# Self-attention: output products in the turned probabilities' banks, values of the last tile one head later, next keys odd first, finer waits at scores and output

## What is computed

```python
def _attn(x, ctx, Wq, Wk, Wv, Wo, bo):       # 16 heads of 64, ctx is the normed x itself
    q = (x @ Wq).reshape(b, n, HEADS, DHEAD)
    k = (ctx @ Wk).reshape(b, m, HEADS, DHEAD)
    v = (ctx @ Wv).reshape(b, m, HEADS, DHEAD)
    scale = DHEAD ** (-0.5)
    sim = jnp.einsum('bihd,bjhd->bhij', q, k) * scale
    attn = jax.nn.softmax(sim, axis=-1)
    out = jnp.einsum('bhij,bjhd->bihd', attn, v).reshape(b, n, INNER)
    return out @ Wo + bo
h = _ln(x, g1, be1)
x = _attn(h, h, Wq1, Wk1, Wv1, Wo1, bo1) + x
```

## Time and profile before

| | us |
|---|---|
| median of three executions | 6849.94 (6849.8 to 6850.25) |
| the profiled execution's own time | 6856.39 |
| its span, first to last instruction | 6854.6 |
| PE busy | 6140.2 (90%) |
| POOL busy | 4645.0 (68%) |
| DVE busy | 5100.9 (74%) |
| ACT busy | 3774.8 (55%) |
| self-attention, first scores of batch 0 to the last addition | about 50 to 1283 |
| mean granted clock of PE | 0.947 of full speed |

### The profile page before, as it was taken

The page is one execution under the profiler, slowest core; times in us unless marked ns, Lnnn a source line. Parts: engine busy times, 40 slices in busy tenths (PEclk is TensorE's granted clock), DMA queues, the critical chain, the costliest instruction groups (busy, mean ns, idle before and its releaser), DMA issues. The chain is left out here.

```text
span 6854.6 us, 73694 instructions
## 1 busy us (share of the span) xinstructions
PE 6140.2 (90%) x20586; PEld 2577.3 (38%) x20586; DVE 5100.9 (74%) x5938; ACT 3774.8 (55%) x6915; POOL 4645.0 (68%) x2164
## 2 busy tenths in 40 slices
PE   9999999999998888888888888888888888888898
PEld 4555555544443332323332323333323333323444
DVE  4444444543218999999999999999999999995623
ACT  4444444432226666666666666666666666664532
POOL 3333334223008999999999999999999999993300
PEclk9999999999999999999999999999999999999998
DMA  2000000213003232333232333232333232332000
GB/s 78 0 0 0 0 0 0 83 25 118 0 0 90 63 87 63 87 79 90 63 87 63 87 79 91 63 87 63 87 79 89 63 87 63 86 79 56 5 0 25
DMA packets 228700, 387.51 MB, mean 57 GB/s; under 512 B 46304, under 2 KB 64416, under 8 KB 225936
## 3 DMA queue, kind: packets, MB, share of 16 engines
q1 hardware_dynamic: 228368, 383.75, 23.0%
HBM read 207.14 MB, written 23.40 MB: 34 GB/s over the span
## 5 line engine op out<-in xcount | busy, mean ns | idle before, releaser
L2580 POOL TENSOR_TENSOR work<-work,weights 128x1024 f32<-128x1024 f32 x1152 | 2693.3, 2366 | 14.0 <-PE banks L2444 7.4
L2444 PE MATMUL banks<-work 128*64 128x512 f32 x4608 | 1359.2, 671 | 554.0 <-POOL work L2585 553.7
L2500 DVE TENSOR_TENSOR_SCAN banks<-banks,work 128x512 f32<-128x512 f32 x1368 | 1710.0, 1271 | 41.6 <-ACT banks L2548 41.3
L2548 ACT ACTIVATE banks<-work 128x512 f32<-128x512 f32 x2304 | 1501.1, 680 | 68.6 <-DVE work L2292 43.1
L2500 DVE TENSOR_TENSOR_SCAN work<-banks,work 128x512 f32<-128x512 f32 x936 | 1173.7, 1270 | 98.3 <-ACT banks L2548 70.9
L2585 POOL TENSOR_TENSOR work<-work,weights 128x1024 f32<-128x1024 f32 x468 | 1104.8, 2361 | 160.4 <-ACT work L2167 160.4
L2005 PE MATMUL banks<-work,weights 128*128 128x512 f32 (+31 forms) x3796 | 1147.3, 453 | 3.6 <-DVE work L2265 3.0
L606 POOL TENSOR_TENSOR work<-work 128x1024 f32<-128x1024 f32 x256 | 480.0, 1895 | 778.8 <-DVE work L472 778.4
L2298 DVE TENSOR_TENSOR work<-banks,weights 128x512 f32<-128x512 f32 x1368 | 902.4, 670 | 0.0
L2005 PEld LDWEIGHTS banks<-work,weights 128*128 128x128 f32 x3796 | 636.5, 190 | 605.1 <-issue 526.5
L2444 PEld LDWEIGHTS banks<-work 128*64 128x64 f32 x4608 | 269.1, 144 | 1414.7 <-POOL work L2585 853.8
(11 more groups left out here) (320 smaller groups left out, 7300.2 us busy)
## 6 DMA issues: line engine op xcount, KB each, us to landing
weights<-mamba_bc SPq DMA_DIRECT2D x592, 256.0 KB, 5.0
work<-work SPq DMA_DIRECT2D x1160, 128.0 KB, 2.3
weights<-mamba_taps SPq DMA_DIRECT2D x5, 2048.0 KB, 7.4
weights<-cross_vo SPq DMA_DIRECT2D x16, 512.0 KB, 6.9
mamba_taps<-work SPq DMA_DIRECT2D x4, 2048.0 KB, 6.8
cross_vo<-weights SPq DMA_DIRECT2D x6, 1024.0 KB, 8.9
work<-in_conv_rows SPq DMA_DIRECT2D x16, 256.0 KB, 5.8
out_T<-X SPq DMA_DIRECT2D x8, 512.0 KB, 3.3
```

What stands on the lines that cost most here:

```text
L2444: mm = e.matmul(ybank[k % 2][64 * h:64 * h + 64, :], fold, ring_pair(n, j)[:, h, :], start=False, stop=(a == SP_ - 1))
L2500: e.tensor_tensor_scan(ub if by_pool(j) else da, da, ub, state[:, i:i + 1], ALU.mult, ALU.add).then_inc(scanned, 1)
L2548: e.activation(banks[:, slot_of(i), :], dt_rep[:, k % 2, h, :], ACT.Exp, scale=decay[:, f:f + 1]).then_inc(da_full, 1)
L2580: e.tensor_tensor(ring_pair(n, j), u_rep[:, k % 2], bc[:, a, 0, :].unsqueeze(1).to_broadcast([P, 2, TC]), ALU.mult) \
```

## The change

Five things, all in `self_attention`:

- The output products' tiles go to banks 4 and 5 and have their own semaphore `out_full`; the additions raise `added` instead of `v_free`, and the first `turn` of the next batch waits for it. `V_SHARE` counts two uses of lane V fewer.
- Ahead of the scores PE waits for `V(-1)` and `S(-1)`, all but the last use of each lane; the wait for all of them stands in the first `mix`.
- `VALUES_AT` is a table from beat to token tiles: tiles 0 and 1 in beat 0, tile 2 in beat 1, tile 3 in beat 2 (behind that beat's second turn). DVE and ACT follow the same table.
- The next batch's first four key tiles are made in the order 1, 0, 3, 2.
- Ahead of the output products PE waits for all but the last use of lane S; the product with k = 7 of the first tile waits for the last.

```diff
@@ -284,17 +284,18 @@
     p_ready = core.sem("self_probs")
     t_full = core.sem("self_t_full")
     tv_free, ts_free = core.sem("self_tv_free"), core.sem("self_ts_free")
+    out_full, added = core.sem("self_out"), core.sem("self_added")
     x_in = lambda b: [(P, core.X[:, k, b, PRE:S1]) for k in range(KD)]
     rows = [P] * KD
 
 
     MEAN_HEAD, VARIANCE_HEAD, BIAS_HEADS = 3, 9, (11, 13)
-    KEYS_AHEAD, KEYS_HEAD, VALUES_AT, V_TAKES = 4, H0 - 2, (0, 1), {3: 0, 7: 2, 11: 4, 14: 6}
+    KEYS_AHEAD, KEYS_HEAD, VALUES_AT, V_TAKES = 4, H0 - 2, {0: (0, 1), 1: (2,), 2: (3,)}, {3: 0, 7: 2, 11: 4, 14: 6}
     V_BEGIN, S_BEGIN = 1 + KEYS_AHEAD // 2, 1 + KEYS_AHEAD // 2
-    V_SHARE, S_SHARE = 12 + PAIRS // 2 + 1 + 2, 12 + PAIRS // 2 + 1
+    V_SHARE, S_SHARE = 12 + PAIRS // 2 + 1, 12 + PAIRS // 2 + 1
     v_done = lambda b: b * V_SHARE + (V_BEGIN + 12 - KEYS_AHEAD // 2 + (MEAN_HEAD + 1) // 4 + 1)
     s_done = lambda b: b * S_SHARE + (S_BEGIN + 12 - KEYS_AHEAD // 2 + VARIANCE_HEAD // 4 + 1)
-    out_bank = lambda m: (core.lane_v, core.banks[:, 4, :])[m]
+    out_bank = lambda m: core.banks[:, 4 + m, :]
 
     with core.nc.Block() as block:
         @block.sync
@@ -355,10 +356,13 @@
                     project(wq, m)
                 for m in range(KEYS_AHEAD, 8):
                     project(wk, m)
-                e.wait_ge(ln.v_free, V())
-                e.wait_ge(ln.s_free, S())
+                e.wait_ge(ln.v_free, V(-1))
+                e.wait_ge(ln.s_free, S(-1))
 
                 def mix(g):
+                    if g == 0:
+                        e.wait_ge(ln.v_free, V())
+                        e.wait_ge(ln.s_free, S())
                     e.wait_ge(tv_free, b * (2 * H0) + 2 * (g + 1))
                     e.wait_ge(ts_free, b * (2 * H0) + 2 * (g + 1))
                     lane, free, full, c = lanes[g // 2 % 2]
@@ -376,6 +380,8 @@
 
                 def turn(g, u):
                     e.wait_ge(p_ready, b * (H0 * UNITS) + (g * UNITS + u + 1))
+                    if g == 0 and u == 0:
+                        e.wait_ge(added, b * KD)
                     for j in range(2):
                         e.wait_ge((tv_free, ts_free)[j], b * (2 * H0) + (2 * g + u))
                         for kt in range(4):
@@ -405,8 +411,8 @@
                     if g >= 1:
                         mix(g - 1)
                     if h in VALUES_AT:
-                        for t in range(2):
-                            project_values(2 * VALUES_AT.index(h) + t)
+                        for t in VALUES_AT[h]:
+                            project_values(t)
                     if g < 0:
                         continue
                     if more and g == MEAN_HEAD:
@@ -415,16 +421,17 @@
                         norm_variance_pe(e, core, nm, ln, S, b + 1, x_in(b + 1), core.mean_d, squared, T)
                     if more and g == KEYS_HEAD:
                         e.wait_ge(nm.ready, b + 2)
-                        for m in range(KEYS_AHEAD):
+                        for m in (1, 0, 3, 2):
                             project(wk, m)
                 mix(H0 - 1)
                 e.wait_ge(ln.v_free, V())
-                e.wait_ge(ln.s_free, S())
+                e.wait_ge(ln.s_free, S(-1))
                 for m in range(KD):
                     for k in range(8):
+                        if m == 0 and k == 7:
+                            e.wait_ge(ln.s_free, S())
                         mm = e.matmul(out_bank(m), wo[:, k, m * P:(m + 1) * P], q[:, k, :], start=(k == 0), stop=(k == 7))
-                    mm.then_inc(ln.v_full, 1)
-                    V.add()
+                    mm.then_inc(out_full, 1)
 
             batches(e, body)
 
@@ -488,7 +495,7 @@
                     if h < H0:
                         reciprocal(h, 0)
                     if h in VALUES_AT:
-                        for t in range(2 * VALUES_AT.index(h), 2 * VALUES_AT.index(h) + 2):
+                        for t in VALUES_AT[h]:
                             e.wait_ge(ln.v_full, V(1))
                             e.tensor_copy(v_[:, t, 0:512], core.lane_v).then_inc(ln.v_free, 1)
                             V.add()
@@ -506,11 +513,10 @@
                                                           in1=core.lane_s, op0=ALU.mult, op1=ALU.mult)
                         last.then_inc(ln.s_free, 1)
                 for m in range(KD):
-                    e.wait_ge(ln.v_full, V(1))
+                    e.wait_ge(out_full, b * KD + m + 1)
                     x = core.X[:, m, b, PRE:S1]
                     e.scalar_tensor_tensor(out=x, in0=out_bank(m), scalar=core.v("bo1", m), in1=x,
-                                           op0=ALU.add, op1=ALU.add).then_inc(ln.v_free, 1)
-                    V.add()
+                                           op0=ALU.add, op1=ALU.add).then_inc(added, 1)
 
             batches(e, body)
 
```

## The result

| | us |
|---|---|
| before, median of 4 executions | 6850.09 (6849.8 to 6860.37) |
| changed, median of 4 executions | 6814.43 (6810.55 to 6822.56) |
| ratio changed to before | 0.9943, 95% interval 0.9931 to 0.9956 |
| changed, the profiled execution | 6822.56, span 6820.7 |

What follows compares the result with a forecast made beforehand. PE was taken to bound the self-attention, so only its gaps could shrink. The sum 7 x 1.23 + 8 x 0.76 + 8 x 1.52 + 7 x 0.61 + 8 x 0.77 = 37.4 us took 6849.94 to 6812.5; range 6805 to 6823.

Steps and rivals of the forecast that it cites:

- (a): Output products in banks 4 and 5: next batch's queries no longer wait for DVE's additions; 1.23 us, seven times.
- (c): Values of tile 3 moved to head 2, between two turns, so the second no longer waits for DVE; 1.52 us, eight times.
- slow restart: At a turn that follows a wait: 0.03 us extra, counted within the gain of (c).
- rival 1: Only part comes: the second turn at (c) still waits, leaving 25.2 us gained, 6824.7 us; chance 0.06.
- (b): Scores wait only for the last key but one, not ACT's copy of key tile 7; 0.76 us, eight times.
- (e): Output products start before ACT has taken the last pair; 0.77 us, eight times.
- (d): Next batch's keys in the order 1, 0, 3, 2: gain 0.86, net 0.61 us after DVE's delay, seven times.
- DVE's delay at head 15: DVE copies the last key before its turned copy, so PE's turn waits 0.25 us longer; taken off (d).
- the idle column: Pricing waits by PE's recorded idle time alone: 34.2 us, 32.4 after DVE's delay, the lower bound; time 6817.5.
- Rival 3: The waits only move: PE arrives earlier at the probabilities and waits for POOL; 6837.5 us if two thirds eaten; chance 0.04.
- Rival 4: Gaps at (a) and (e) are the queue's own and stay: 22.6 us gained, 6827.3 us; chance 0.03.
- the sign of being wrong on the whole: Behind the self-attention's barrier: a stage changing by more than 4 us would show the whole forecast wrong.

Runs made afterwards that it cites:

- both waits covered: The mix of head 13 put between head 14's turns, keys 3 and 2 between head 15's, against the changed kernel; median 6806.24 us.

## Why the prediction was right

The bound, the five places and their prices held. Per batch the forecast was 4.89 us and the trace shows 4.97. That the median came within 2 us of 6812.5 is in part luck: the four executions of the changed kernel spread over 12.0 us, two profiles of it differ by 0.4 us in the self-attention and by 5.1 behind it, and a longer wait for the loads in batch 0 (1.4 us) was not in the sum. The length of a batch is what bears the forecast out.

- (a) 1.23 forecast, 1.22 by undoing it. (c) 1.52 and 1.52; the 0.03 of slow restart in it has no row, and the turn behind the wait shows 0.02 (0.99 us to the next start, from 389.70 to 390.69, against 0.97 for such a turn without a wait). DVE and ACT had the margin that the rows promised: DVE's turned copy ahead of the second turn was done 2.1 us early, and rival 1 did not come.
- (b) 0.76 and (e) 0.77: by undoing them 0.85 and 0.83, in the longer form of the wait. At their places in the two timelines they fit: from the output products to the scores 36.51 us became 34.53, 1.98 less where (a) and (b) have 1.99 together, and the last mix's step fell from 4.37 to 3.61, 0.76.
- (d) 0.61 forecast, 0.71 measured. The step that was mis-sized is DVE's delay at head 15, 0.25 on record and 0.16 in the trace. I had put the key's copy and the turned copy end to end. In the timeline of DVE in the changed kernel they overlap by 0.08, the second starting before the first one's recorded end:

```profile
470.22 0.69 DVE L446 COPY work<-banks 128x512 f32<-128x512 f32 x1 [2.74 <-PE banks L331]
470.83 0.68 DVE L463 COPY work<-banks 128x512 f32<-128x512 f32 x1
```

- The two ways to price a wait, by starts or by the idle column, differed by 5 us. The batch decides for the starts: 4.97 per batch, where the idle column of one batch gives 1.33 + 0.44 + 0.96 + 0.70 + 0.69 + 0.79 before, less 0.60 at head 15 now, 4.3. The Trainium skill (Trainium Kernel Development and Optimization, Performance Expectations) calls matmul busy time a bad metric for the distance to roofline because matmuls are pipelined. The trace agrees that busy times overlap: 322.93 + 14.00 reaches 0.17 us past the next block's start. I then forgot this in the expectation for the two covered waits, which was 0.47 us per batch too low.
- The sum over the stage: 7 x (1.22 + 0.71) + 8 x (0.76 + 1.52 + 0.77) = 37.9, less 1.4 for the longer wait for the loads in batch 0, 36.5. The next stage's first matmul moved from 1283.84 to 1247.50, 36.3 us.
- Rival 3 had the wait for POOL grow. It stayed at 3.5 us in 8. That this is because the chain starts with PE's own scores is argued and not tested. Rival 4 fell with parts (a) and (e) undone, where the waits for DVE and ACT came back with their full length.

What the forecast had too small is the scatter of the other stages, for which I allowed 4 us. It took the 0.45 us between three executions for a sign of less, although the profiled execution lay 6.45 above their median. Over 13 profiles of 11 kernels with the same code behind the barrier, the rest of the program, from the next stage's first matmul to the end of the span, took between 5563.7 and 5573.2 us. Most of that is the last stage: from its first matmul to the end 84.5 or 84.6 us in seven profiles, 77.5 to 78.1 in six. It is not the program. The kernel with both waits covered was profiled twice and showed 84.5 once and 77.6 once; PE's timelines of one round of the last stage in these two profiles, the longer one first:

```profile
6745.00 3.70 PE L1614 MATMUL banks<-X,mean_d 128*128 128x512 f32 x8
6750.56 6.31 PE L1626 MATMUL banks<-weights,work 128*128 128x64 f32 x32 [1.86 <-DVE work L1667]
6756.66 3.52 PE L1634 MATMUL banks<-mean_d,work 128*128 128x1 f32 x16
```

```profile
6747.54 4.88 PE L1614 MATMUL banks<-X,mean_d 128*128 128x512 f32 x8
6753.10 3.76 PE L1626 MATMUL banks<-weights,work 128*128 128x64 f32 x32 [0.68 <-DVE work L1667]
6756.69 1.90 PE L1634 MATMUL banks<-mean_d,work 128*128 128x1 f32 x16
```

By stretches, granted clock third from the end of a row, the longer one first:

```profile
6751.00:6757.00 6.00, 6.00 (x32) 6.00 (x32) 2.34 (x4) 1.56 (x2) 2.96 (x2) 0.53 0.00 0
```

```profile
6753.00:6757.00 4.00, 3.90 (x36) 3.93 (x36) 2.87 (x4) 2.10 (x2) 2.88 (x2) 1.00 0.00 0
```

The two have their stretches at 1.2 GHz at different work. In the shorter one the clock is low for the first part of L1614 (granted clock 0.51 from 6747 to 6750 us) and full for L1626 and L1634; in the longer one it is the other way round (1.00 from 6745 to 6748). The block L1626 waits for DVE (L1667) and starts 5.56 us after L1614 in both, so slow passes in L1614 only shorten PE's idle time, 0.68 instead of 1.86 us, while slow passes in L1626 and L1634 add their whole length: 6.10 + 3.38 us from start to start where the other has 3.59 + 1.76. So what a drop of the clock costs depends on whether it falls on work that another engine's wait hides; why it fell at other work in one execution than in the other stays open. The Trainium skill (TensorE: Matmul & The Clock Gate, Part 1) has the gate's window run freely; the trace agrees in that the same program has its drops at other work, L1614 once and L1626 once. The scatter of this stage also means that the sign of being wrong on the whole, a later stage that changes by more than 4 us, cannot tell the change from chance: this stage changes by 7 us between two profiles of one kernel.

## What to carry to other kernels

Where one engine is busy for 97% of a stage, list its waits by place, price each by the distance between starts, and look for work of the same engine that can stand between the wait and what it waits for: five small edits gave 4.97 us per batch, and two more 1.57. Cover is spent where it stands, so here one piece in each of two places was worth more than two pieces in either. And a wait for "all uses of a buffer" deserves a look at which use the next instruction really needs.

## What I had not expected

Keys placed between two turns cost nothing for the change of shape: such a turn takes 0.88 us (462.82 to 463.70 in the kernel with the waits covered), against 0.97 with a mix behind it (467.13 to 468.10) and 1.02 between scores and a mix. So the order of blocks is worth a tenth or two of a us per batch by itself. The same wait cost 0.69 us in one form of the program and 0.78 in another, although releaser and released were the same, and both forms stand in the kernel before. And the wait for the loads in batch 0, on data that its queries do not need, was anywhere between 0.2 and 4.0 us long in kernels that load the same, and 0.5 and 1.6 us in two profiles of one kernel.
